# Fusing a dot product, sharing one widened copy and widening ten comparisons in an edge-sorting phase

## The reference, cut to what matters

```python
# layer 1: the part of the attention logit that comes from the edge's 128 features
e = edge_attr @ We.T + be
a = leaky_relu(sum((h[src] + e) * attn, axis=-1), 0.01)
# = leaky_relu(h[src] @ attn + edge_attr @ (We.T @ attn) + be @ attn)
# layers 0 and 3: out = segment_sum(h[src] * norm, dst)                  -> a matrix of edge counts
# layer 2:
a_in  = segment_sum(feat_in[src]  * iw[:, None], dst)                    # sums of edge_weight
a_out = segment_sum(feat_out[dst] * ow[:, None], src)                    # sums of edge_weight_n2
```

## Time and profile before

| | us |
|---|---|
| median of 3 runs | 4699.41 |
| lowest and highest | 4694.25, 4701.1 |
| the profiled execution, its own time | 4693.42 |
| its span, first to last instruction | 4691.6 |

### The profile page before, as it was taken

One profiled execution on the slowest core, in us unless ns is written; L12 is line 12 of the kernel. 1 busy time (PEld: TensorE's weight loads), 2 busy tenths in 40 slices (PEclk: granted clock), 3 DMA queues, 4 the chain that ended last, 5 costly groups with the idle time before them and its releaser, 6 DMA issues. The chain is left out here.

```text
span 4691.6 us, 87142 instructions
## 1 busy us (share of the span) xinstructions
PE 3560.4 (76%) x19416; PEld 2666.4 (57%) x19417; DVE 2729.4 (58%) x7745; ACT 1686.2 (36%) x5377; POOL 1202.6 (26%) x828
## 2 busy tenths in 40 slices
PE   5555557888887767999983333589999699998978
PEld 4333335777776666888862222577888444444444
DVE  7999999999987771112237777677766300000523
ACT  1444442234444440000017776577776100000110
POOL 1888888888888100000000000000000000000000
PEclk9999999999998888999985555899999899999989
DMA  2333333567767664444445544343332153442064
GB/s 102 102 102 102 101 97 86 149 177 209 218 204 241 243 237 120 134 120 144 134 112 173 162 157 151 121 140 123 117 97 76 36 208 129 160 153 79 1 249 137
DMA packets 435571, 656.93 MB, mean 140 GB/s; under 512 B 97532, under 2 KB 291767, under 8 KB 435362
## 3 DMA queue, kind: packets, MB, share of 16 engines
q1 hardware_dynamic: 354306, 526.63, 36.2%
q10 hardware_dynamic: 53040, 121.95, 7.2%
q0 software_dynamic: 28144, 7.36, 2.5%
HBM read 438.84 MB, written 216.02 MB: 140 GB/s over the span
## 5 line engine op out<-in xcount | busy, mean ns | idle before, releaser
L989 POOL DMA_INDIRECT slots<-all_B,put_index x800 | 1179.2, 1474 | 345.7 <-issue 240.8
L1725 POOL DMA_DIRECT2D out_dram<-all_B x7 | 8.5, 1221 | 2242.2 <-DVE all_B L1709 2242.2
L965 PE MATMUL put_ps<-put_right_in,put_left_in 128*128 128x125 f32 x2380 | 351.6, 298 | 138.6 <-ACT put_left_in L835 138.2
L765 DVE TENSOR_SCALAR put_hot<-all_iota_bf,put_words_in 128x125 bf16<-128x125 bf16 x2400 | 445.3, 315 | 3.3 <-DMA put_words_in<-slots 3.3
L1220 PE MATMUL lm_ps<-lm_v,lm_node 125*128 x1220 | 170.0, 184 | 328.4 <-DVEq L1087 127.3
L1185 ACT ACTIVATE lm_raised<-lm_hot,srt_words 128x125 f32<-128x125 bf16 x1200 | 360.3, 385 | 140.2 <-DVE lm_top L1100 64.6
L965 PEld LDWEIGHTS put_ps<-put_right_in,put_left_in 128*128 128x128 f32 x2380 | 307.1, 204 | 167.8 <-ACT put_left_in L835 157.4
L835 ACT CAST put_left_in<-put_hot 128x640 f32 (+1 forms) x238 | 172.5, 725 | 629.6 <-issue 321.8
L2262 DVE TENSOR_TENSOR upd_pre<-upd_po,upd_bias 125x512 f32<-125x512 f32 x25 | 17.3, 692 | 630.5 <-PE upd_po L2193 630.5
L1835 PE MATMUL att_ps<-att_right,att_left 128*125 128x125 f32 x2380 | 318.7, 286 | 68.4 <-ACT att_right L1856 64.6
L969 PE MATMUL put_ps<-put_right_out,put_left_out 128*128 128x125 f32 x2380 | 342.7, 297 | 0.0
(11 more groups left out here) (346 smaller groups left out, 5955.9 us busy)
## 6 DMA issues: line engine op xcount, KB each, us to landing
c_T<-counts SPq DMA_DIRECT2D x255, 312.5 KB, 2.9
pair<-put_T ACTq DMA_DIRECT2D x125, 625.0 KB
hot<-put_hot SPq DMA_DIRECT2D x480, 160.0 KB
att_ring<-hot SPq DMA_DIRECT2D x240, 320.0 KB, 3.2
all_A<-in_edge_attr_dram SPq DMA_DIRECT2D x100, 448.0 KB
lm_planes<-src_rows SPq DMA_DIRECT2D x123, 320.0 KB, 3.7
counts<-put_T ACTq DMA_DIRECT2D x125, 312.5 KB
lm_hot<-hot SPq DMA_DIRECT2D x120, 320.0 KB, 3.0
```

The source lines that it names most:

```text
L765: ins = v.tensor_scalar(hot[:, h, t, c * S:c * S + P], k["iota_bf"][:, :], words_in[:, j, c, t:t + 1], None, ALU.is_equal)
L965: ins = t_.matmul(tile(1, c), left_in[:, c, :], right_in[:, c, :], start=False, stop=False, skip_group_check=True)
L989: nc.gpsimd.indirect_dma_start(slots, bass.IndirectOffsetOnAxis(index[:, C * g + j:C * g + j + 1], 0), stage[:, C * g + j, :], None).then_ ...
```

## The change

It has three parts.

1. In `edge_dot` the multiply and the reduce are replaced by eight `tensor_tensor_reduce`, one for each of the 8 edges of a partition, of 128 elements each, with the sum in an accumulator that goes to one column of `dot`. The semaphore `multiplied` is gone; SyncE's load waits for `dotted`.
2. `left_in` and `right_out` are replaced by one fp32 copy `wide` of SRC's one-hots, which ACT makes. It is the stationary side of the `iw` product and the moving side of the `ow` product; the weight `ow` now multiplies DST's one-hots in `left_out`. DVE's copy L772 and multiply L773 become one multiply. ACT's copy waits for `summed_out` of the unit before, where it waited for `summed_in`.
3. The ten comparisons of a unit become two `tensor_tensor` of 625 elements.

```diff
-        left_in, left_out = b.sb("left_in", [L, HALF, S]), b.sb("left_out", [L, HALF, S])
-        right_in, right_out = b.sb("right_in", [L, HALF, P]), b.sb("right_out", [L, HALF, P])
+        wide = b.sb("wide", [L, HALF, S])
+        right_in, left_out = b.sb("right_in", [L, HALF, P]), b.sb("left_out", [L, HALF, S])
...
-                        sp.wait_ge(multiplied, g - 1 + HEAD)
+                        sp.wait_ge(dotted, g - 1 + HEAD)
...
                     dve.wait_ge(loaded[h], 32 * (2 * i + u // 2) + 32)
-                    v.tensor_tensor(prod[:, h, :, :], ea[:, h, :, :], f["vrow"][:, :].unsqueeze(1).to_broadcast([P, C, DE]),
-                                    ALU.mult).then_inc(multiplied, 1)
-                    dve.wait_ge(multiplied, g + 1 + HEAD)
                     dve.wait_ge(staged, g - 3 + HEAD)
-                    v.tensor_reduce(dot[:, u, :], prod[:, h, :, :], AX.X, ALU.add).then_inc(dotted, 1)
+                    for c in range(C):
+                        ins = v.tensor_tensor_reduce(prod[:, h, c, :], ea[:, h, c, :], f["vrow"][:, :], 1.0, 0.0, ALU.mult, ALU.add,
+                                                     dot[:, u, c:c + 1])
+                    ins.then_inc(dotted, 1)
...
                         for t in (SRC, DST):
-                            for c in range(HALF):
-                                ins = v.tensor_scalar(hot[:, h, t, c * S:c * S + P], k["iota_bf"][:, :], words_in[:, j, c, t:t + 1],
-                                                      None, ALU.is_equal)
+                            ins = v.tensor_tensor(hot_of[:, h, t, :, 0:P], k["iota_bf"][:, :].unsqueeze(1).to_broadcast([L, HALF, P]),
+                                                  field(t), ALU.is_equal)
...
                         dve.wait_ge(summed_out, u + 1)
-                        v.tensor_copy(left_out[:, :, :], hot_of[:, h, DST, :, :])
-                        v.tensor_tensor(right_out[:, :, :], hot_of[:, h, SRC, :, 0:P], field(WOUT), ALU.mult).then_inc(outs, 1)
+                        v.tensor_tensor(left_out[:, :, :], hot_of[:, h, DST, :, :], words_in[:, j, :, WOUT].unsqueeze(2).to_broadcast([L, HALF, S]),
+                                        ALU.mult).then_inc(outs, 1)
...
                     act.wait_ge(hots, u + 1)
-                    act.wait_ge(summed_in, u + 1)
-                    nc.scalar.copy(left_in[:, :, :].rearrange("p c n -> p (c n)"),
+                    act.wait_ge(summed_out, u + 1)
+                    nc.scalar.copy(wide[:, :, :].rearrange("p c n -> p (c n)"),
                                    hot[:, ds(u % SLOT, 1), SRC, :].rearrange("p a n -> p (a n)")).then_inc(cast, 1)
...
-                            ins = t_.matmul(tile(1, c), left_in[:, c, :], right_in[:, c, :], start=False, stop=False, skip_group_check=True)
+                            ins = t_.matmul(tile(1, c), wide[:, c, :], right_in[:, c, :], start=False, stop=False, skip_group_check=True)
...
-                            ins = t_.matmul(tile(2, c), left_out[:, c, :], right_out[:, c, :], start=False, stop=False, skip_group_check=True)
+                            ins = t_.matmul(tile(2, c), left_out[:, c, :], wide[:, c, 0:P], start=False, stop=False, skip_group_check=True)
```

More of the change, by code:

```diff
@@ L528, in phase_front @@
         blocks_in, loaded = [b.sem(f"blocks_in{h}") for h in range(2)], [b.sem(f"loaded{h}") for h in range(2)]
-        based, cols_hot, rows_hot, multiplied, dotted, picked, placed = (
-            b.sem(n) for n in ("based", "cols_hot", "rows_hot", "multiplied", "dotted", "picked", "placed"))
+        based, cols_hot, rows_hot, dotted, picked, placed = (
+            b.sem(n) for n in ("based", "cols_hot", "rows_hot", "dotted", "picked", "placed"))
         counted, carried, negated, looked = (b.sem(n) for n in ("counted", "carried", "negated", "looked"))
@@ L677, in turn @@
                             place(chain, i, 0)
-                for sem in (rows_hot, cols_hot, multiplied, dotted, picked, placed):
+                for sem in (rows_hot, cols_hot, dotted, picked, placed):
                     dve.sem_inc(sem, HEAD)
```

## The result

| | before, us | after, us |
|---|---|---|
| median | 4696.83 (4 runs) | 4778.67 (4 runs) |
| lowest and highest | 4693.02, 4701.1 | 4775.54, 4786.33 |
| the profiled execution's span | 4691.6 | 4784.5 |

The ratio is 1.0176, with a 95% interval of 1.0159 to 1.0194: the changed kernel is 82 us slower. The forecast had the sign and not the size; it said +36.

The account below looks back on a forecast made before the run. DVE was taken to bound the first loop, DVE and ACT together the second. +2 us (dot product), +30 (ring) and +4 (clock) on the 4699.4 us median gave 4735 us, range 4697 to 4800 us.

Parts of the forecast that it names:

- the intervals with an evacuation: Second loop, from one ACT copy to the next with an evacuation between: 124 of them, set by ACT, staying at 5.2 us.
- the price of the pair: First loop, fused instruction plus accumulator read on DVE: 0.30 us, eight 2.40 us against 2.38, +2 us in all.
- the lower bound of -14: First loop, eight pairs at 0.21 and 0.07 us each: 2.24 us a group, -14 us.
- Parts 2 and 3 on DVE: Second loop: DVE's work falls from 3.8 to about 3.0 us a unit and stops being the bound between evacuations.
- The ring: Second loop, closed chain of ACT's copy, `iw` and `ow` matmuls: 3.50 us, lengthening intervals without an evacuation, +30 us.
- The clock: Second loop: the ring's 2.50 us of matmuls slow with PE's earlier granted clock, 14 us at most, +4 us added.
- The dear fused instruction: Rival, first loop: read doesn't overlap or half rate, +88 or +106 us, 4821 or 4841 us; 18 in 100.
- a gain through ACT's intervals: Rival, second loop: intervals with an evacuation hang on DVE and shrink, at most 211 us less, 4524 us; 10 in 100.
- the dear rival's halfway figure: The time if the fused instruction in the first loop is dear by half: 4780 us.

Follow-up runs that it names:

- the shorter chain on ACT: Kernel before with fused dot product and wide comparisons but no shared copy, plus the record-column copy L837 moved from ACT to DVE: 4602.38 us, ratio 0.9797.
- part 3 alone: Kernel before with only the ten comparisons of a unit made into two wide ones: 4673.07 us, ratio 0.9951.
- PE kept busy: Changed kernel with seven more bf16 matmuls of zeros on PE at the start of each block of units: 4684.28 us, ratio to before 0.9965.
- parts 1 and 3: Kernel before with fused dot product and wide comparisons, without the shared copy and its later wait on ACT: 4629.91 us, ratio 0.9857.

## Why the prediction was right and wrong

**What bounds the kernel.** Right. DVE sets the pace of the first loop: the loop got 0.51 us a group shorter for 0.68 us less in the dot product, and the rest is accounted for by DVE's own instructions that wait for POOL. The prediction didn't look at POOL at all, though the wide multiply that it removed had been holding POOL up. In the second loop the intervals with an evacuation are ACT's, by the experiment with the shorter chain on ACT, and the others were in good part DVE's, by part 3 alone, which took 20 us off.

**Part 1.** The step that failed is the price of the pair. The fused instruction's own 0.21 us, from the line through the earlier trace rows, was exact. The read was put at 0.09 us from ACT's pair and takes nothing. The sum's term was +2 us; the eight pairs gave -68 us, instructions that wait for POOL took most of the difference back, and -51 is far outside the lower bound of -14, since that bound also gave the read 0.07 us. The row at hand was the earlier trace rows: it shows where the read starts and not when the next instruction may start, and the prediction filled that with another engine's habit. The fused instruction doesn't run at half rate: 128 elements take 0.21 us from start to start. The rule that the prediction cites from the Trainium skill, page "Vector Engine (DVE) Microarchitecture Reference", section "Points that are easy to get wrong", is stated for the scalar-tensor-tensor shape, and this instruction of another kind doesn't behave so.

**Parts 2 and 3 on DVE.** Right. A wide comparison takes 0.81 us and two 1.52; DVE's work in the loop fell by 160 us, and it waits for PE in each unit.

**The ring.** Right in its place and its length: 3.50 forecast, 3.51 measured. Its cost at full clock was put at +30 us; with PE kept busy the loop was 44 us longer than before, with some of the lower clock left in it, and the estimate at that run comes to about 30. One of the sums behind the 30 is slightly off: with 5.25 us for the intervals with an evacuation it gives 113 x 3.50 - (1017 - 124 x 5.25) = 29.5 us, not 31.

**The intervals with an evacuation.** Forecast to stay at 5.2; they went from 5.15 to 5.30 us, and back to 5.15 with PE kept busy. With the half clock a ring takes 5.1 us and outlasts ACT's 4.9. That was wrong by 124 x 0.15 = 19 us. How much of it is the clock's isn't shown, since part 3 alone and parts 1 and 3, without a ring, have 5.25 too.

**The clock.** This is the step that failed in size. The prediction multiplied the ring's 2.50 us of matmuls by the clock granted *before*, 14 us at most, and added 4. The change itself set the clock: it turned an idle time of PE that had been spread over a pair of units into one of 2.4 us at each evacuation, and the matmuls behind it ran at 1.2 GHz on the very ring that the change had closed. This cost at least 96 us, which the experiment that kept PE busy gave back, and about 111 by the estimate there, where the term was +4. The prediction never asked how long PE would stand idle at an evacuation, though its own rows had the answer: the next copy comes 4.9 us after the last, and the ring leaves PE with 2.5 us of matmuls in it. What such idle times do to the clock those rows didn't show: behind 2.58 us of it the ten matmuls there took 1.38 us.

**The sum.** Forecast +2 (part 1), +30 (ring), +4 (clock). Measured -51 for part 1, +141 for ring and clock together, and +3 us in phases behind, the last not explained. Of the 141 the added matmuls took 96 away, and the estimate gives 30 to the ring and the remaining 111 to the lower clock, with whatever else lengthened the intervals with an evacuation. So the first term was 53 us too high, the clock's 107 us too low by that estimate, and the ring's about right. That the time fell into the stated range is luck: the first and the third error have opposite signs, and with the third alone it would have been above 4800 us.

**The rivals.** The dear fused instruction didn't happen, nor did a gain through ACT's intervals. None of the rivals was the clock, which is what decided. That the dear rival's halfway figure, 4780 us, is nearly the measured time is chance.

## What to carry to other kernels

When a change puts a wait between two engines, draw the closed ring of waits that it makes, take its length from rows, and then ask what the engines do while they wait in the longest step beside it. If TensorE stands idle there, its next matmuls may run at half the clock, and they are now on the ring: the clock of the kernel before is no price for the kernel after. A buffer that is shared to save an engine's work is paid for on another engine, and is worth nothing when the saved engine stops being the bound at once.

## What the runs showed of the hardware

- On DVE the accumulator read behind a fused multiply-and-sum is free when another one follows: eight of 128 fp32 elements take 1.70 us, 0.21 each, which is 0.07 us and 1.04 ns an element, the same as a plain instruction.
- PE's granted clock fell with how idle PE was, and not by one idle time: ten matmuls took over 1.9 us (2.50 at the lower clock) in place of 1.38 behind 55 of 66 idle times over 2.2 us in the changed kernel, and behind 2 of 9 in the kernel before. Matmuls that only add zeros count as activity: with them the loop's clock rose from 0.85 to 0.98, and it got 96 us shorter. How much activity it takes, the runs don't tell.
- DVE and POOL's issue of an indirect DMA hold each other up, by the kind of DVE instruction. The wide fp32 multiply (two inputs in SBUF) stretched an issue of 1.19 us to up to 3.4. The fused multiply-and-sum, which reads two fp32 operands too, didn't (1.18 to 1.26 us). A tensor_scalar of 0.18 us took 0.28 to 0.62, mostly 0.60, when it started over 0.54 us into an issue (47 of 47), and a scalar_tensor_tensor of the same size wasn't lengthened there (0 of 43).
- In the three kernels with wide comparisons, without part 2 and with ACT's queue as it was, the intervals with an evacuation are 5.25 to 5.27 us on the mean, against 5.15 before, at clocks of 0.92 to 0.97 against 0.93. Why wasn't followed up.
